# A routed transformer block on one core: fewer place tables ahead of the stage boundary, centring spread out, and identity transposes while TensorE waits

## What is computed

```python
# 1: gated attention; 16 query heads of 128 over 8 groups, fp8-rounded inputs
ln = layernorm(x)
q, qx, k, v = [fp8(ln / s) * s @ w.T * ws for each of wq, wqx, wk, wv]   # q, k normalised per head
kx, vx = split(ctx @ w_kv_x.T)                                          # kx normalised per head
core, xout = softmax(q k^T) v, softmax(qx kx^T) vx
x1 = x + tanh(g_xattn) * (fp8(concat(core, xout) / smooth) @ wproj.T * scale)
# 2: mixture of 8 experts, the best two for each token
hat = layernorm(x1)
probs = softmax(30 * tanh(hat @ w_gate / 30)); best two of 8
out = x1 + tanh(g_ffn) * sum_e probs_e * (silu(hat @ w1[e]) * (hat @ w3[e])) @ w2[e]
```

## Time and profile before

| | |
|---|---|
| median of three runs | 714.76 us |
| profiled execution, its own time | 714.06 us |
| its span, first to last instruction | 712.2 us |
| PE busy | 643.2 us, 90% |
| DVE, ACT, POOL busy | 605.3, 549.0, 461.8 us (85%, 77%, 65%) |
| granted TensorE clock, mean over the span | 0.962 |
| attention steps with PE almost always busy | about 62 to 520 us |
| seam | about 558 to 565 us |
| first slot under way to the end | about 577 to 712 us |

### The profile page before, as it was taken

How to read it: one execution, slowest core, us unless ns; L and a number is a source line. 1 busy time by engine, 2 the same in 40 slices (tenths; PEclk the granted TensorE clock), 3 DMA queues, 4 the chain that set the end, 5 groups by cost and what they waited for, 6 DMA issues and landing times. The chain is left out here.

```text
span 712.2 us, 14919 instructions
## 1 busy us (share of the span) xinstructions
PE 643.2 (90%) x4548; PEld 587.6 (83%) x4549; DVE 605.3 (85%) x1389; ACT 549.0 (77%) x1925; POOL 461.8 (65%) x648
## 2 busy tenths in 40 slices
PE   1678999999999999999999999999987259999995
PEld 0677889999998999999899999999976248888884
DVE  7679899999989999998999999888897486777772
ACT  4887889989988998998899899888873136666571
POOL 4567677787777778877777887786563523445442
PEclk9969999999999999999999999999999559999999
DMA  7201200011020001101000110100293612323322
GB/s 219 59 1 31 60 1 30 2 60 31 1 61 1 30 2 60 31 1 60 1 32 2 53 42 1 60 1 2 89 397 136 214 30 40 54 48 52 51 41 27
DMA packets 35509, 37.72 MB, mean 53 GB/s; under 512 B 2704, under 2 KB 30352, under 8 KB 35440
## 3 DMA queue, kind: packets, MB, share of 16 engines
q1 hardware_dynamic: 31024, 30.84, 13.3%
q0 software_dynamic: 4416, 6.03, 5.2%
HBM read 31.62 MB, written 5.24 MB: 52 GB/s over the span
## 5 line engine op out<-in xcount | busy, mean ns | idle before, releaser
L1410 POOL TENSOR_SCALAR shared<-shared,rsum 128x256 f32<-128x256 f32 x256 | 142.4, 568 | 59.7 <-DVE rsum L984 54.2
L693 ACT ACTIVATE shared<-s,nmax 128x256 f32<-128x256 f32 x256 | 122.1, 498 | 29.0 <-DVE nmax L979 28.9
L1404 POOL TENSOR_TENSOR rstd<-rstd,half 128x7 f32<-128x7 f32 (+1 forms) x64 | 90.7, 1417 | 5.3
L979 DVE TENSOR_REDUCE nmax<-s 128x2 f32<-128x512 f32 x128 | 86.7, 680 | 2.9 <-PE s L376 2.4
L989 DVE TENSOR_TENSOR pt_lo<-t,pt_hi 128x512 fp32r<-128x512 f32 x124 | 84.2, 679 | 4.0 <-ACT pt_hi L701 3.0
L709 ACT ACTIVATE shared<-route_bank,head_w 128x512 f32<-128x512 f32 (+1 forms) x124 | 81.4, 688 | 0.0
L701 ACT CAST pt_hi<-t 128x512 fp32r<-128x512 f32 x124 | 74.1, 597 | 9.5 <-PE t L391 6.9
L391 PE MATMUL t<-ident,shared 128*128 128x128 f32 x496 | 76.2, 277 | 5.6 <-DVE v_lo L959 2.3
L974 DVE TENSOR_TENSOR qk_lo<-shared,qk_hi 128x512 fp32r<-128x512 f32 x96 | 78.3, 816 | 3.1 <-POOL qk_hi L1421 2.0
L376 PE MATMUL s<-qk_hi 128*128 128x256 f32 x256 | 78.0, 305 | 1.1 <-ACT shared L693 0.9
L1952 DVE TENSOR_TENSOR w_lo<-expert_w,w_hi 128x1024 fp32r<-128x1024 f32 x46 | 56.2, 1225 | 25.2 <-ACT w_hi L1834 24.5
(11 more groups left out here) (270 smaller groups left out, 1951.5 us busy)
## 6 DMA issues: line engine op xcount, KB each, us to landing
expert_w<-in_w SPq DMA_DIRECT2D x24, 512.0 KB, 9.1
spare<-in_wT SPq DMA_DIRECT2D x19, 256.0 KB, 3.0
wp_raw<-in_wpT SPq DMA_DIRECT2D x16, 256.0 KB, 2.9
spare<-in_wkvT SPq DMA_DIRECT2D x16, 128.0 KB, 3.2
spare<-in_wT SPq DMA_DIRECT2D x9, 128.0 KB, 3.2
spare<-in_x SPq DMA_DIRECT2D x1, 1024.0 KB, 5.6
x_hat<-acc SPq DMA_DIRECT2D x1, 1024.0 KB, 4.6
out<-spare SPq DMA_DIRECT2D x1, 1024.0 KB, 8.0
```

The source lines that it names most:

```text
L693: e = act.activation(probs[:, st, h * S:(h + 1) * S], s_bank[st][:, h * S:(h + 1) * S], ACT.Exp, bias=nmax[:, st, h:h + 1], accum_out=psum ...
L979: dve.tensor_reduce(nmax[:, st, :], s_bank[st][:].rearrange("p (h t) -> p h t", h=2), AX, ALU.max, negate=True).then_inc(max_done, 1)
L1404: pool.tensor_tensor(rstd[:, st, c], rstd[:, st, c], half[:, c], ALU.pow).then_inc(rstd_ready, 1)
L1410: m = pool.tensor_scalar(probs[:, st, c], probs[:, st, c], rsum[:, st, h:h + 1], 1.0, ALU.mult, ALU.mult)
```

## The change

It has these parts:

1. **Fewer early tables.** POOL makes the tables of tiles 0 and 1 in `attention` (4 instead of 12) and those of tiles 2 and 3 at the beginning of its list in `experts`. The tables of tiles 4 to 7 are made by DVE (L1907 doubles its columns). `first_places` covers four tiles and waits for the first count alone.
2. **Order of the tail.** `choose` is split into `find_top` and the rest; the rest of part 0 moves behind `x1_normalise(3)`. On PE `turn_hat(2)` moves behind the last output projection, and `rank(0)` behind `turn_hat(4)`, `rank(1)` behind `logits(4)`. The last expert's w1 and w3 are loaded ahead of the stores, behind the sum of unit 27, and w2 behind the last projection.
3. **Order in experts.** The 48 scale products (`find_scales`) move from ahead of slot 0 to behind its `hidden`, `find_fill` moves into step 0, and DVE makes `scale_slot` behind the rests for slot 0.
4. **Identity transposes.** PE transposes the identity 14 times at the start of `experts`, and 24 times behind the token products (`turn_idle`). Nothing reads the result.
5. **Centring.** Group 1 is summed, centred and split in the start, so unit 1 has no such work; for later groups the first four blocks are centred two at place 0 and two at place 2, and the rest at place 1.
6. **The start.** Chunk 1 of the rows is normalised on ACT (`row_scale(1)`, with a shift from POOL) instead of DVE.
7. **Widening.** POOL's `widen(u - 1, b1, 0)` moves behind `power(u + 2, 0)` and `scale_probs(u, 0, 1)`.

The diff, cut to its core ("..." stands for lines left out; eight spaces of indent are taken away):

```diff
 tile_out, counted = sem("tile_out"), sem("counted")
-place_chain, early_placed = sem("place_chain"), sem("early_placed")
+place_chain, early_placed, tops_found = sem("place_chain"), sem("early_placed"), sem("tops_found")
...
     sp.dma_start(x1, x.rearrange("b (s p) h -> p (b s) h", p=P)).then_inc(x_reloaded, 16)
-    def load_expert(e):
+    def load_expert(e, some=(0, 1, 2)):
...
         at = expert_w[:, 3 * e * n:3 * (e + 1) * n]
-        for i, w in enumerate((w1, w3, w2)):
+        for i in some:
+            w = (w1, w3, w2)[i]
...
         load_expert(e)
+    sp.wait_ge(acc_read, 4 * (G - 1))
+    load_expert(E - 1, (0, 1))
+    sp.wait_ge(tile_out, ST)
+    load_expert(E - 1, (2,))
...
     sp.dma_start(out.rearrange("b (s p) h -> p (b s) h", p=P), x1).then_inc(route.sums_begun, 16)
-    sp.wait_ge(tile_out, ST)
-    load_expert(E - 1)
...
             pe.wait_ge(aff_done, 3 * U)
+        if part == 1:
+            pe.wait_ge(place_chain, 1)
...
     logits(1)
-    turn_hat(2)
...
     out_project(G - 1, 1, 3, 31, 1, s_bank[1][:, 0:H])
+    turn_hat(2)
...
     turn_hat(3)
+    turn_hat(4)
     rank(0)
-    turn_hat(4)
     logits(3)
+    logits(4)
     rank(1)
-    logits(4)
...
+    def row_scale(c):
+
+        act.wait_ge(ln_shift, c)
+        for t in range(*chunks[c]):
+            m = act.activation(acc[:, t, :], acc[:, t, :], ACT.Identity, scale=lnr[:, t:t + 1], bias=ln_mr[:, t:t + 1])
+        m.then_inc(z_ready, 1)
...
         affine_in(n)
+    row_scale(1)
...
     square(1)
-    act.wait_ge(ln_shift, 1)
-    for t in range(*chunks[2]):
-        m = act.activation(acc[:, t, :], acc[:, t, :], ACT.Identity, scale=lnr[:, t:t + 1], bias=ln_mr[:, t:t + 1])
-    m.then_inc(z_ready, 1)
+    row_scale(2)
...
     square(2)
+    weights_hi(1, 1, 0)
+    weights_hi(1, 1, 1)
...
+    weights_hi(1, 1, 2)
+    weights_hi(1, 1, 3)
...
-        if g + 1 < G and b < 2:
-            c = 2 * b + place if g > 0 else (b - 1) * 9 + 2 * place
-            for n in ((c,) if g > 0 else (c, c + 1)):
-                if 0 <= n < 4:
-                    weights_hi(g + 1, (g + 1) % 2, n)
+        if 0 < g < G - 1 and b < 2:
+            weights_hi(g + 1, (g + 1) % 2, 2 * b + place)
...
     quantise_in(0, 4)
-    row_normalise(1)
...
     dve.tensor_tensor(v0_w[:, 1], v0_raw, v0_w[:, 0].bitcast(F32), ALU.subtract).then_inc(v0_ready, 1)
+    for k in range(KT):
+        sum_weights(1, k)
+    centre_weights(1, 0, (0, 1, 2, 3) + later_blocks(1))
...
     normalise_kv(0, 0, 0, early_banks[0][1])
+    centre_weights(1, 1, (0, 1, 2, 3))
...
     split_heads(0, 0, 1)
+    centre_weights(1, 1, later_blocks(1))
...
     row_sum(0, 0, 1)
+    weights_lo(1, 1, 0)
+    weights_lo(1, 1, 1)
...
     row_sum(0, 1, 1)
-    for k in range(KT):
-        sum_weights(1, k)
-    centre_weights(1, 0, (0, 1, 2, 3))
+    weights_lo(1, 1, 2)
+    weights_lo(1, 1, 3)
...
     rest_v0(1, s_bank[1])
-    centre_weights(1, 0, later_blocks(1))
...
-        centring = 1 if g == 0 else 0
-        if place in (0, 2) and g + 1 < G and b == centring:
-            centre_weights(g + 1, 1, (0, 1, 2, 3) if place == 0 else later_blocks(g + 1))
-        if place in (0, 2) and g + 2 < G and b == 3:
-            centre_weights(g + 2, 0, (0, 1, 2, 3) if place == 0 else later_blocks(g + 2))
+        parts = {0: (0, 1), 2: (2, 3)}
+        if place in (0, 2, 1) and 0 < g < G - 1 and b == 0:
+            centre_weights(g + 1, 1, parts[place] if place in parts else later_blocks(g + 1))
+        if place in (0, 2, 1) and g + 2 < G and b == 3:
+            centre_weights(g + 2, 0, parts[place] if place in parts else later_blocks(g + 2))
...
             sum_weights(g + 2, place - 2)
-        if place in (1, 3) and g + 1 < G and b < 2:
-            for c in (((), (0, 1)), ((2,), (3,)))[b][place // 2] if g > 0 else ((0, 1), (2, 3))[place // 2]:
+        if place in (1, 3) and 0 < g < G - 1 and b < 2:
+            for c in (((), (0, 1)), ((2,), (3,)))[b][place // 2]:
...
-    def choose(part):
+    def find_top(part):
...
         tiles = RANKED[part]
-        n, c = len(tiles), slice(tiles[0], tiles[-1] + 1)
-        lanes = route.table[:, T_LANE:T_LANE + E].rearrange("p (o e) -> p o e", o=1).broadcast_to([P, n, E])
...
             m = dve.max_index(route.top_i[:, t, :], route.top[:, t, :], route.cap[:, t, :])
-        link(m)
+        m.then_inc(tops_found, 1)
+
+    def choose(part):
+
+        tiles = RANKED[part]
+        n, c = len(tiles), slice(tiles[0], tiles[-1] + 1)
+        lanes = route.table[:, T_LANE:T_LANE + E].rearrange("p (o e) -> p o e", o=1).broadcast_to([P, n, E])
+        dve.wait_ge(tops_found, part + 1)
...
-        dve.wait_ge(counted, 2)
-        n = NT - ST
+        dve.wait_ge(counted, 1)
+        n = len(RANKED[0])
...
     x1_normalise(2)
-    choose(0)
+    find_top(0)
...
     x1_normalise(3)
+    choose(0)
     x1_normalise(4)
+    find_top(1)
...
     first_places()
+    find_top(2)
...
-    def row_shift():
-
-        t = slice(*chunks[2])
-        pool.wait_ge(ln_rstd, 3)
+    def row_shift(c):
+
+        t = slice(*chunks[c])
+        pool.wait_ge(ln_rstd, c + 1)
         pool.tensor_tensor(ln_mr[:, t], mv[:, t, 0], lnr[:, t], ALU.mult).then_inc(ln_shift_part, 1)
-        pool.wait_ge(ln_shift_part, 1)
+        pool.wait_ge(ln_shift_part, c)
...
     row_power(1)
+    row_shift(1)
...
     row_power(2)
-    row_shift()
+    row_shift(2)
...
             heads_hi(u + 1, bh, 0)
-        if above(u, 0):
-            widen(u - 1, b1, 0)
...
         scale_probs(u, 0, 1)
+        if above(u, 0):
+            widen(u - 1, b1, 0)
...
     pool.wait_ge(early_placed, 1)
-    for t in range(NT - ST):
+    for t in range(0, 2):
...
 row_place = sb("row_place", [P, TOP * NT])
-at_place = early_tiles(early, NT, E)[0]
+at_place, _, early_row, _ = early_tiles(early, NT, E)
...
+    def turn_idle(times):
+
+        for _ in range(times):
+            pe.transpose(h1_bank[0][:, 0:P], ident[:], ident[:])
+
+    turn_idle(14)
     pe.wait_ge(identified, 1)
-    pe.wait_ge(route.places_set, 1)
+    pe.wait_ge(route.places_set, 2)
...
     for i, (j, t) in enumerate(order):
-        if i == len(order) - QUARTER:
+        if i == len(order) // 2:
...
-
-    pe.wait_ge(weighed, 1)
-    for n in range(TOP * NT):
-        for part in range(3):
-            m = pe.matmul(y_bank[0][:, 0:SLOTS], at_place[:, n // NT, n % NT, :], scale_slot[:, part, n, :],
-                          start=n == 0 and part == 0, stop=n == TOP * NT - 1 and part == 2)
-    m.then_inc(scales_found, 1)
+    turn_idle(24)
+
+    def find_scales():
+
+        pe.wait_ge(weighed, 1)
+        for n in range(TOP * NT):
+            for part in range(3):
+                m = pe.matmul(y_bank[0][:, 0:SLOTS], at_place[:, n // NT, n % NT, :], scale_slot[:, part, n, :],
+                              start=n == 0 and part == 0, stop=n == TOP * NT - 1 and part == 2)
+        m.then_inc(scales_found, 1)
...
     hidden(0, 0, 1)
-    find_fill()
+    find_scales()
...
     def step(n, par):
-        if isinstance(n, int) and n == 0:
-            pe.wait_ge(scales_known, 1)
-            pe.wait_ge(tokens_known, 1)
...
             hidden(n + 1, 1 - par, 1)
+        if isinstance(n, int) and n == 0:
+            find_fill()
+            pe.wait_ge(scales_known, 1)
+            pe.wait_ge(tokens_known, 1)
...
     m.then_inc(identified, 1)
-    last_place = row_place[:].rearrange("p (j t) -> p j t", j=TOP)[:, :, NT - 2:NT]
+    last_place = row_place[:].rearrange("p (j t) -> p j t", j=TOP)[:, :, NT // 2:NT]
     for j in range(TOP):
-        m = dve.tensor_tensor(at_place[:, j, NT - 2:NT], table[:, T_PLACE:T_PLACE + P].rearrange("p (o r) -> p o r", o=1).broadcast_to([P, 2, P]),
-                              last_place[:, j].rearrange("p (n o) -> p n o", o=1).broadcast_to([P, 2, P]), ALU.is_equal)
+        m = dve.tensor_tensor(at_place[:, j, NT // 2:NT], table[:, T_PLACE:T_PLACE + P].rearrange("p (o r) -> p o r", o=1)
+                              .broadcast_to([P, NT // 2, P]),
+                              last_place[:, j].rearrange("p (n o) -> p n o", o=1).broadcast_to([P, NT // 2, P]), ALU.is_equal)
...
     link(dve.tensor_copy(factor_part[:, 2, :], left[:, 1, :]))
-    for part in range(3):
-        m = dve.tensor_tensor(scale_slot[:, part], at_slot[:], over_slots(factor_part[:, part, :]), ALU.mult)
-    m.then_inc(weighed, 1)
+
+    def slot_scales():
+
+        dve.wait_ge(routed, chain[0])
+        for part in range(3):
+            m = dve.tensor_tensor(scale_slot[:, part], at_slot[:], over_slots(factor_part[:, part, :]), ALU.mult)
+        m.then_inc(weighed, 1)
...
     rows_rest(0, 0)
+    last_rows()
+    slot_scales()
+    e = expert_of(1)
+    weights_rest(1, 1, e, 0)
+    rows_rest(1, 1)
+    weights_rest(1, 1, e, 1)
+    fill_places()
+    fill_table()
...
     dve.tensor_copy(row_scale[:], y_bank[0][:, 0:SLOTS]).then_inc(scales_known, 1)
-    last_rows()
-    fill_places()
```

(12 more changed lines are left out.)

## The result

The changed kernel takes 701.94 us (median of four runs, 700.40 to 703.93); the kernel before takes 714.43 (four runs). The ratio is 0.983, with a 95% interval of 0.980 to 0.986. The profiled execution took 701.43 us, its span is 699.5, and the mean granted clock is 0.971. The prediction was 701.1 us, in a range of 698.0 to 706.5. It took 13.7 us off the median of the first three runs, 714.76; the medians differ by 12.5 us.

What follows compares the result with a forecast made beforehand. PE bounds the steady steps, POOL's tables the seam, a DVE chain the way to slot 0. Seam and slot 0 -8.5, steady -1.8, unit 1 -2.9, start -0.5: 714.76 - 13.7 = 701.1 us, range 698 to 706.5.

Steps and rivals of the forecast that it cites:

- The seam: From attention to experts: DVE's start, held by POOL's tables, comes at 558.1 instead of 564.88, 6.8 us sooner.
- Both terms: At the seam: POOL keeps 4 of 12 tables, 0.70 us each, and starts them 1.2 us sooner.
- Seam to slot 0: DVE chain: slot_token ends 6.1 us behind the seam, take_hidden(0, 0) 14.7 later; turn_hidden stands at 578.9 instead of 588.46.
- The wait put in at 0.9 us: Ahead of slot 0, DVE's rows_rest(0, 0) waits for gathered rows turned by PE and copied by ACT: nothing to 1.7 us.
- Given back: Behind slot 0's turn_hidden: find_fill 0.6 us at most, out_rows_known with queued rests about 0.4 us; +1.0 us.
- The identity transposes: On PE early in experts: cost nothing to a little, little expected of the clock either way.
- The rival at 0.14: Clock low for slot 0, as transposes don't count or PE stands still: 1.7 us lost, 702.8 us; chance 0.14.
- Steady steps: Behind 84 us: fewer blocks at place 0 bring normalise_q sooner; 2.3 won, 0.5 given back: -1.8 us (0 to -2.6).
- at most what those waits hold: Steady steps are bound by PE, so the gain is limited to PE's waits, 2.6 us behind 84 us.
- moving `widen`: nothing: In the units: 0.6 us of POOL work goes behind rstd and a scaling, needed only at the unit's end: nothing.
- The start and unit 1: Start -0.5 us (chunk 1 off DVE, group 1's work added); unit 1 -2.9 us from PE's waits between 62 and 84 us.
- 1.32 us off in front of the first rests, on which PE's first projection waits: At the start: DVE no longer normalises chunk 1, so PE's first projection starts near 19 us.

Runs made afterwards that it cites:

- Experiment 2: Changed kernel with all twelve tables made on POOL ahead of the seam again and DVE making two tiles behind it: 709.19 us, ratio 0.992.
- experiment 5: Changed kernel with group 1's sums, centring and weight splitting back where the kernel before had them, in unit 1: 701.09 us, ratio 0.981.
- 1: Changed kernel with row chunk 1 normalised on DVE again instead of ACT: 703.79 us, ratio 0.984.
- 3: Changed kernel without the 38 idle identity transposes on PE: 702.18 us, ratio 0.983.
- 6: Changed kernel with centring of groups 1 and on back to four blocks at one place, widening still late: 705.52 us, ratio 0.987.
- 7: Changed kernel with only POOL's widening back ahead of its second scaling: 699.30 us, ratio 0.980.
- 8: Changed kernel with the slot scales (DVE's and PE's parts) found ahead of slot 0's rows again: 701.29 us, ratio 0.983.
- 12: Changed kernel with widening, group 1 and scales back, take_hidden(0, 0) ahead of fill_places, and chunk 2's statistics ahead of weights_lo: 696.96 us, ratio 0.976.

## Why the prediction was right

**The seam** (-6.8 predicted, -6.50 measured, with 1.0 us of chance between runs of the same instructions). Both terms held: the tables take 5.54 us less on POOL (5.6 in the sum), and start 1.06 us sooner behind accumulation 30 (1.2 in the sum) by the earlier chain of `choose` and `first_places`; PE and POOL end within 0.13 us of each other. Experiment 2 shows the first term by itself; the order of the tail was not tried alone.

**Seam to slot 0** (-2.7, measured -2.81). `slot_token` at 6.1 was 6.35 by its end, and 14.7 was 14.15. The wait put in at 0.9 us was 1.06, but its cause was mis-named: ScalarE's split of the weights, not the gathered rows. What the prediction left unsaid is which of the two moves pays: alone, the fill (1.6 us) and not the scales; the other 2 us were not tried by themselves.

**Given back** (+1.0, measured +0.93). The place was right: 0.70 us of it lie between the turns of slots 0 and 1, with `find_fill`'s products and a wait of 0.51 us for the rests. That the size met the forecast is luck. The changed kernel's profile is the lowest of seven with these instructions; the other six lie 1.4 to 4.1 us above the one profile of the kernel before.

**The identity transposes** (nothing). Right to 0.64 us in the trace, nothing in the medians. The rival at 0.14 had the clock low for slot 0. The granted clock did fall to 0.50 from 567.2 to 570.2 us, and the DVE chain covered it: PE's products of the first two slots were done by 574.15 us, ahead of `hid` at 574.56.

**Steady steps** (-1.8, at most -2.6; measured -3.06). The step that failed is the bound "at most what those waits hold": the spread centring gave 4.0 us, of which 2.6 are the waits of PE that were read. The weight loads' waits for the same two tiles of VectorE held 6.2 us (4.5 and 1.7) and fell to 1.6. And "moving `widen`: nothing" was wrong by 0.9 us the other way. The two errors leave 1.3 us.

**The start and unit 1** (-0.5 and -2.9, together -3.4; measured -0.45, or -1.55 when the later landing is taken off). From 62 to 84 us PE's waits fell from 3.8 to 1.0 us, as forecast. The start failed in two steps. The first projection came at 22.0 us, not 19, because the step "1.32 us off in front of the first rests, on which PE's first projection waits" looked at one of two inputs. GpSimd's widenings were the other, and taking the 1.32 us away put the rests straight behind the conversions, where they shut GpSimd out. And `normalise_q(0)` came at 31.5 us, behind the 30 beyond which the forecast called itself wrong (30.4 when the later landing is taken off). Here the step was to lay group 1's work into a wait for `rstd` of 3.54 us: it stands behind VectorE's wait for ScalarE, and by experiment 5 only 1.38 us of waiting were left for its 3.53 us. These 2.15 us ate what the move gave in unit 1.

So of the total of -13.7 against -12.7, the seam and slot 0 (-8.5 predicted, -8.38 measured) were right for their reasons, though the last term by luck in its size; start and unit 1 were short by some 2 us, and the steady steps and the stretch from accumulation 25 to 30 made up most of it. That stretch is luck too: from 25 to 29 it lost 0.5 us, as all runs with the late widening do, and between 29 and 30 it won 1.3 us with the granted clock at 1.00 instead of 0.86, before and then after:

```profile
529.37:541.20 11.83, 9.70 (x56) 8.31 (x55) 10.06 (x24) 6.45 (x20) 6.65 (x13) 0.86 0.98 365
```
```profile
526.34:536.88 10.54, 8.42 (x56) 7.05 (x55) 9.71 (x24) 6.34 (x20) 7.06 (x13) 1.00 1.06 400
```

With the same instructions there, six of the twelve experiments (1, 3, 6, 7, 8, 12) took 10.5 to 10.7 us and the other six 11.8 or 11.9. (The third number from the end of a row is the granted clock.)

## What to carry to other kernels

Where an engine waits for two inputs, cost both producers and ask what the edit puts beside each; here a shorter queue on VectorE made GpSimd's work the later one. When edits go in together in a steady loop, take them out singly and in pairs: one of the two here was a loss that the other hid, and leaving it out is part of a version that is 5 us faster. A long block cut in pieces can give more than the waits that PE's own row names: read the row of its weight loads beside it.

## What the runs showed that was not expected

- GpSimd's widening of 128x512 f16 took 0.61 us alone and 4.42 us when VectorE had conversions and then five subtractions with two float32 inputs queued back to back: it didn't get in between them.
- The other way round, VectorE's conversion (L1008) took 0.28 us in most places and up to 1.25 us beside GpSimd's two-input subtraction.
- Idle transposes by the identity raise TensorE's clock. In the changed kernel's windows (us, busy PE, PEld, DVE, ACT and POOL, clock, DMA share, GB/s):

```profile
559.70:564.10 4.40, 4.40 (x30) 4.24 (x26) 3.02 (x13) 1.99 (x2) 2.20 (x2) 0.61 0.09 30
564.20:566.30 2.10, 0.41 (x2) 0.20 (x2) 2.10 (x4) 1.05 (x2) 1.09 (x1) 1.00 0.20 62
...
567.20:570.20 3.00, 3.00 (x10) 2.19 (x9) 2.96 (x6) 1.28 (x3) 0.71 (x1) 0.50 0.15 44
```

In the first window 24 of PE's 30 products were transposes, and in it the clock rose from 1.2 GHz to 2.4 (a mean of 0.61, and 1.00 right behind it); without them it stayed at 0.50 from 560 to 570 us. The rule that the prediction cited from the Trainium skill (TensorE: Matmul & The Clock Gate, Part 4: PE-mode transpose) does not hold for these float32 transposes. PE then stood for most of 2.1 us, and the clock fell again once slot 0 had begun.
